# Expert blocks in three host steps instead of four, with the hidden transposes between the two ups of the next pair

## What is computed

```python
scores = sigmoid(xf @ gate_w.T)
_, sel = top_k(scores + expert_bias[None, :], K)          # K = 2 of E = 8
top_scores = take_along_axis(scores, sel, axis=1)
rin = xf[tok_idx] * sc_sorted[:, None]                     # rows in the order of their expert
for e in range(E):
    h = silu(rin @ w1[e].T) * (rin @ w3[e].T)
    out_sorted = out_sorted + m * (h @ w2[e].T)
routed = zeros((N, D)).at[tok_idx].add(out_sorted)
shared = silu(xf @ sw1.T) * (xf @ sw3.T) @ sw2.T
return routed + shared
```

## Time and profile before

| | |
|---|---|
| three runs | 507.58, 510.66, 513.54 us |
| median | 510.66 us |
| the profiled execution | 508.22 us (span of its instructions 506.4 us) |
| busy share of the span | TensorE 89%, VectorE 69%, ScalarE 49%, GpSimd 34% |
| TensorE, mean granted clock | 0.974 of full speed |
| DMA | 42.02 MB, mean 83 GB/s |

### The profile page before, as it was taken

The page is one execution under the profiler, slowest core; times in us unless marked ns, Lnnn a source line. Parts: engine busy times, 40 slices in busy tenths (PEclk is TensorE's granted clock), DMA queues, the critical chain, the costliest instruction groups (busy, mean ns, idle before and its releaser), DMA issues. The chain is left out here.

```text
span 506.4 us, 7287 instructions
## 1 busy us (share of the span) xinstructions
PE 450.3 (89%) x2162; PEld 356.1 (70%) x2162; DVE 347.2 (69%) x994; ACT 247.2 (49%) x479; POOL 173.8 (34%) x181
## 2 busy tenths in 40 slices
PE   2769799589989999999999998998998899899991
PEld 1447588458668776888778786887776688788860
DVE  6968569988486964577978967888778354621173
ACT  2868264223577377455044416360751544955540
POOL 3787232354022333400000000060525015477771
PEclk9999799789999999999999999999999899999997
DMA  8421212002000000980000000142323223346494
GB/s 306 164 80 57 62 33 80 5 20 83 1 1 2 0 1 0 293 218 0 1 2 1 0 2 0 32 136 74 119 71 112 88 79 111 105 150 191 123 380 138
DMA packets 32966, 42.02 MB, mean 83 GB/s; under 512 B 3483, under 2 KB 26781, under 8 KB 32928
## 3 DMA queue, kind: packets, MB, share of 16 engines
q1 hardware_dynamic: 28224, 32.28, 21.0%
q0 software_dynamic: 3744, 8.42, 4.5%
q10 hardware_dynamic: 960, 0.86, 0.5%
HBM read 24.97 MB, written 18.39 MB: 86 GB/s over the span
## 5 line engine op out<-in xcount | busy, mean ns | idle before, releaser
L678 PE MATMUL acc<-w_down,act_s 128*128 128x256 f32 x384 | 91.5, 384 | 0.9 <-DVE act_s L1410 0.9
L678 PEld LDWEIGHTS acc<-w_down,act_s 128*128 128x128 f32 x384 | 73.6, 193 | 12.8 <-DVE act_s L1410 1.3
L654 PE MATMUL ring<-xt_h,up_l 128*128 128x512 f32 x160 | 71.1, 444 | 1.4 <-DVE kv_sum L1490 1.4
L1137 ACT ACTIVATE act_s<-ring 128x512 f32<-128x512 f32 x48 | 28.6, 596 | 73.5 <-PE ring L656 73.3
L655 PE MATMUL ring<-xt_l,up_h 128*128 128x512 f32 x160 | 63.4, 396 | 0.0
L656 PE MATMUL ring<-xt_h,up_h 128*128 128x512 f32 x160 | 63.3, 395 | 0.0
L1625 POOL TENSOR_TENSOR rstd<-var_eps,minus_half 128x4 f32<-128x4 f32 x14 | 14.5, 1039 | 135.7 <-DVE var_eps L1225 135.7
L717 PE MATMUL ring<-up_e,act_s 128*128 x184 | 45.7, 392 | 2.3 <-issue 2.0
L1677 POOL DMA_INDIRECT x_rows<-main_a,slots x32 | 31.1, 972 | 43.7 <-ACT main_a L1158 34.8
L1414 DVE TENSOR_TENSOR act_s<-ring,act_s 128x512 f32<-128x512 f32 x32 | 21.9, 686 | 34.3 <-ACT act_s L1137 16.4
L717 PEld LDWEIGHTS ring<-up_e,act_s 128*128 128x128 f32 x184 | 34.2, 196 | 7.2 <-issue 3.2
(11 more groups left out here) (281 smaller groups left out, 1009.6 us busy)
## 6 DMA issues: line engine op xcount, KB each, us to landing
main_b<-x_rows SPq DMA_DIRECT2D x22, 257.0 KB, 3.0
x_rows<-v_t SPq DMA_DIRECT2D x1, 3983.5 KB, 16.1
up_l<-y_rows SPq DMA_DIRECT2D x5, 512.0 KB, 5.9
stage<-in_w_mlp SPq DMA_DIRECT2D x8, 256.0 KB, 2.6
up_e<-in_w_moe SPq DMA_DIRECT2D x8, 256.0 KB, 2.6
x_rows<-v_t SPq DMA_DIRECT2D x1, 1927.5 KB, 22.4
x_nat<-in_x SPq DMA_DIRECT2D x7, 256.0 KB, 7.9
out_x<-x_nat SPq DMA_DIRECT2D x6, 256.0 KB, 5.0
```

Of the source, the lines that this page charges most:

```text
L654: pe.matmul(out, wl, xh, start=first, stop=False, skip_group_check=True)
L678: last = pe.matmul(acc[t // 2][:, t % 2, :], act_s[n % RING][:, tok], w_down[:, u, :], start=u == 0 and t % 2 == 0, stop=final, skip_group ...
L1137: act.activation(act_s[n % RING][:, :], bank[:, :], ACT.Silu).then_inc(free_sem((step, "A", u)), 1)
```

## The change

The downs of a pair, their copy and their store come one host step earlier, so a pair goes through three steps (x transposed; ups; hidden transposes and downs) instead of four, and step 26 is gone from the list. On TensorE, the hidden transposes of pair n-2 stand between the ups of block 0 and block 1 of pair n-1, and the downs of pair n-2 behind block 1. On ScalarE the copy of the transposed hidden stands ahead of silu, and the copy of the downs (now pair n-2) behind it. GpSimd stores pair n-2.

```diff
-    gather 0 4 5, blk 0 26, moe 3 1, shared 3 0 1, fetch_tile 1 0 1 2 3, gather_tile 1 0 1 2 3"""
+    gather 0 4 5, moe 3 1, shared 3 0 1, fetch_tile 1 0 1 2 3, gather_tile 1 0 1 2 3"""
...
-            def block_ups(n, experts):
...
+            def block_up_rows(n, j, e, bank):
+
+                for c in range(C):
+                    last = pe.matmul(bank[:, j * 2 * P:(j + 1) * 2 * P], x_block_t[n % 2][:, c, j * P:(j + 1) * P],
+                                     up_e[:, bass.ds(e * UP + c * 2 * P, 2 * P)], start=c == 0, stop=c == C - 1)
+                return last
...
                         experts[n - 1] = [block_expert(n - 1, j) for j in range(pair_blocks(n - 1))]
-                        block_ups(n - 1, experts[n - 1])
-                    if 2 <= n <= PAIRS + 1:
+                        freed(pe, (("blk", n - 1), "T"))
+                        key = (("blk", n - 1), "U")
+                        bank = open_bank(key)
+                        last = block_up_rows(n - 1, 0, experts[n - 1][0], bank)
+                        if n >= 2:
+                            transpose_hidden(n - 2)
+                        if pair_blocks(n - 1) == 2:
+                            last = block_up_rows(n - 1, 1, experts[n - 1][1], bank)
+                        close_bank(key, last)
+                    elif n > PAIRS:
                         transpose_hidden(n - 2)
-                    if n >= 3:
-                        block_downs(n - 3, experts[n - 3])
+                    if n >= 2:
+                        block_downs(n - 2, experts[n - 2])
...
+                    if n >= 2:
+                        key = (("blk", n - 2), "H")
+                        bank = full(act, key)
+                        if n >= 4:
+                            full(act, (("blk", n - 4), "D"))
+                        wide = pair_blocks(n - 2) * P
+                        act.activation(hid_block_t[n % 2][:, 0:wide], bank[:, 0:wide], ACT.Copy).then_inc(free_sem(key), 1)
                     if 1 <= n <= PAIRS:
                         bank = full(act, (("blk", n - 1), "U"))
...
-                elif kind == "blk" and part >= 3:
-                    n = part - 3
+                elif kind == "blk" and part >= 2:
+                    n = part - 2
```

More of the change, by code:

```diff
@@ L1180, in _ @@
                                        ACT.Silu).then_inc(block_silu, 1)
-                    if 2 <= n <= PAIRS + 1:
-                        key = (("blk", n - 2), "H")
+                    if n >= 2:
+                        key = (("blk", n - 2), "D")
                         bank = full(act, key)
[L1184 to L1195, removed]
+                        if n >= RESULTS + 2:
+                            blocks = sum(pair_blocks(m) for m in range((n - 2) % RESULTS, n - 2, RESULTS))
+                            act.wait_ge(y_sent[(n - 2) % RESULTS], 16 * blocks)
+                        wide = pair_blocks(n - 2) * D
+                        act.activation(y_blocks[(n - 2) % RESULTS][:, 0:wide], bank[:, 0:wide], ACT.Copy,
                                        scale=gates[:, 3:4]).then_inc(free_sem(key), 1)
```

## The result

| | before | changed |
|---|---|---|
| runs | 507.58, 510.66, 513.54, 505.84 us | 520.65, 517.70, 518.07, 516.16 us |
| median | 509.12 us | 517.88 us |
| profiled execution | 508.22 us (span 506.4) | 520.65 us (span 518.8) |

The change makes the kernel slower: ratio 1.018, 95% interval 1.0135 to 1.0233, that is 9.4 us (6.9 to 11.9) of 509.12. The sign is clear of the noise; whether it is more or less than 2% is not settled.

What follows compares the result with a forecast made beforehand. TensorE's pace and GpSimd's backlog were taken to bound the end together. Delays of 3.4, 4.4, 0.9 and 1.6 made 10.3 us; 3.2 given back left 7.15, so 515.4, plus 2.44 to the median: 517.8 us, range 509.0 to 521.0.

Steps and rivals of the forecast that it cites:

- Two queues at once: At the end GpSimd's backlog holds up to pair 18, TensorE's pace of 3.25 us a pair holds pairs 19 and 20.
- The copy is covered: The second block's ups cover ScalarE's hidden copy with 0.3 us to spare, so the wait costs the matmuls nothing.
- The reads are held by the wait and cost: The downs' new wait stops TensorE's sequencer; two expert-number reads queue behind it, 1.85 us to the next ups' arithmetic.
- Stall 0.44, step 3.69: Each steady expert step on TensorE stalls 0.44 us, so it takes 3.69 us instead of 3.25.
- Ahead of the sends, 1.14: GpSimd's sends start 1.14 us later: 0.7 for one more pair of downs, 0.44 for one stalled interleaved step.
- Step 9, 2.2 us of standing, ups of pair 9 3.4 late: TensorE stands 2.2 us for the hidden copy behind ScalarE's rows; the ups of pair 9 start 3.4 us late.
- Given back by the last steps, 3.2: One step less of latency at the end gives back 3.2 of the 10.3 us of delay.
- The other branch just hidden: The branch behind TensorE's last downs moves by 11.0 us; its additions end at 507.3, just hidden by 508.15.
- The reason given for "held": The wait goes with the downs' register arithmetic, a control instruction, and so stops the sequencer; with a matmul reads would run ahead.
- rival B: The reads run ahead of the wait, steps stay 3.25 us, the kernel is not slower: 509.9 us; chance 0.20.
- Rival D: The main forecast, plus step 9's stand taking TensorE to its lower clock: + 1.7 us, 519.5; chance 0.10.
- Rival C: TensorE never holds GpSimd up, the last store comes 3.4 us earlier: 507.2 us, the ceiling; chance 0.05.

Runs made afterwards that it cites:

- e1: The changed kernel with the next pair's expert numbers read ahead of the wait for the downs, not behind it; ratio to before 1.0043.
- e5: The changed kernel with a small fixed-address matmul put first in the downs' bank to carry the wait for the hidden copy; ratio to before 1.018.
- e9: e1 plus the last four lots of rows in ScalarE's gaps of steps 9 and 10, and single-block hidden transposes ahead of the ups; ratio to before 0.9975.
- e3: e1 plus the rows of the last two tiles filled by ScalarE behind step 9's copies; ratio to before 0.9973.
- e8: As e3, but one of the two tiles' rows behind step 9's copies and the other behind step 10's; ratio to before 0.9979.
- e7: The changed kernel with the hidden transposes behind the ups of both blocks; one run, 533.87 us.

## Why the prediction was right, point by point

The forecast of 517.8 us met 517.88, and that it met it so closely is luck. It went out from a median of 510.66 for the kernel before and added 7.15; the median with the fourth run is 509.12, 1.5 lower, and the change costs 8.8 by the medians, 9.0 in the traces and 9.4 by the ratio. The two errors cancel. The direction, the place and the mechanism held; the size was a fifth too small.

- **Two queues at once** held: after the change GpSimd's backlog is used up by 471 us and TensorE sets the end.
- **The copy is covered**: held, no wait ahead of L732 in a full step, and e1 shows it with the reads out of the way.
- **The reads are held by the wait and cost**: held. On the sequencer of the changed kernel the downs' arithmetic starts at 458.4, the reads at 458.7, the next ups' at 460.4, as the earlier trace rows but now behind the release:

```profile
L732 PEldq FUSED_REGOPS  x2: 46/46/46, 458.4 to 458.5; - x2
...
L708 PEldq TENSOR_LOAD <-block_e x2: 297/416/534, 458.7 to 459.6; - x2
```

- **Stall 0.44, step 3.69**: the term was too small. The ten full steps take 3.68 to 3.94, on average 3.78. The missing 0.09 is the restart: after a stand the ups of one block take 0.96 or 0.97 us (485.95 to 486.92) and not 0.87, because its first record is 478 ns long instead of 379. The row for it was there (the eight of 438.21 in the earlier trace rows take 1.99 us, those of the earlier trace rows 1.89) and I did not price it. From pair 9 to pair 22 that made 7.7 us in place of 6.9.
- **Ahead of the sends, 1.14**: measured 1.36 (sends at t2 + 38.40 against 37.04). The one pair of downs more costs 0.8 rather than 0.7. Step 5 to 6 stood as foreseen (3.72 from ups to ups against 3.25). The restart behind that stand adds the missing 0.1.
- **Step 9, 2.2 us of standing, ups of pair 9 3.4 late**: 1.85 us, and 3.75 late. The stand is shorter since TensorE came later to it: the ups of pair 8 were 1.4 late rather than 1.1, and took the restart on top. The copy ended at t2 + 39.37, which on the clock of the kernel before is 443.54; the prediction has 443.4, though its own terms (442.6, 0.5 and 0.4) add up to 443.5. From there to the ups it took 2.17 us instead of 2.0.

```profile
446.55 0.37 ACT L1183 ACTIVATE k_r<-ring 128x256 f32<-128x256 f32 x1
```

- **Given back by the last steps, 3.2**: too large; it was 2.4 (from the ups of pair 22 to the last store 13.0 us before, 10.6 after). Of the missing 0.8, about 0.3 is the way of the stores: one of them took 1.30 us in place of 0.99. Some 0.2 is lost from the ups of pair 22 to those of pair 23 (3.03 us against 2.81), and another 0.1 is the restart ahead of the downs of pair 22.
- **The other branch just hidden**: held. Its additions and the last store both came later than foreseen (12.6 us for 11.0, and 9.0 for 7.15), and VectorE waited another 1.18 us for the last fetch behind it:

```profile
510.66 1.61 DVE L1248 SCALAR_TENSOR_TENSOR x_nat<-ring,small,x_nat 128x512 f32<-128x512 f32 x2 [1.36 <-PE ring L690]
513.45 0.42 DVE L1583 TENSOR_TENSOR x_nat<-x_nat,gate_pad 128x256 f32<-128x256 f32 x1 [1.18 <-DMA gate_pad<-y_rows]
```

- **The reason given for "held"** was only half right. I had put it on the wait being carried by a control instruction. e5 took that away and the steps stayed as long. So rival B could not have come true on the ground that I gave it; the reads run ahead only if they stand ahead of the wait, as in e1.
- **Rival D** did not come: the granted clock was 1.00 (2.4 GHz) in the stretch from 441 to 507 us of the changed kernel, in spite of the stand of 1.85 us.
- **Rival C's ceiling** of 3.4 us stayed out of reach; e9 got 1.6 of it in its trace.

## What to carry to other kernels

When a pipeline is made one stage shorter, mind not only what the array does during the new wait but what the waiting engine's sequencer still has to do behind it: register reads at 0.65 us each, hidden as long as it runs ahead, come to lie bare behind a fresh wait. Issue such reads ahead of the wait, for the next step; here that one edit took back 8.65 of 9.0 us. And a shorter way pays only where the queue at the end was waiting for it. With the stall gone, three versions (e3, e8, e9) lie 0.2 to 0.3% below the kernel before, each within its interval, so none is shown to be faster; in the traces uncovered copies at the ragged steps gave back part of the 2.6 us (e9).

## What the runs showed that I had not expected

- On TensorE, register arithmetic and reads behind a matmul that waits for a semaphore were held until that wait ended, though they wait for nothing themselves (e5, 470.0 and 470.04, and 24 of 24 pairs).
- The first matmul of the ups after a stand is 478 ns in the records against 379 (all 16 flagged stands of the changed kernel from 405 us on), and what follows the group of four comes 0.09 to 0.1 us later.
- Much of the spread from run to run (505.8 to 513.5 us for the kernel before) can lie outside the changed part. In the profiled executions, with the same work up to there, the transposes of step 2 started anywhere from 402.9 to 409.7 us. Part of it is how long TensorE's clock stays at its lower level of 1.2 GHz near 395. In the changed kernel, around idle spells of 1.25, 0.60, 0.90 and 1.11 us, the granted clock is 0.56 and 0.59 of 2.4 GHz in two stretches,

```profile
396.00:400.00 4.00, 2.89 (x9) 2.19 (x8) 0.79 (x4) 0.60 (x1) 0.00 (x0) 0.56 0.57 158
400.00:404.00 4.00, 4.00 (x12) 3.20 (x11) 0.42 (x1) 2.10 (x3) 0.00 (x0) 0.59 0.00 0
```

against 0.62 and then 0.95 in the kernel before (394 to 398 and 398 to 402). From the ups of pair 0 to the transposes of step 2 it takes 8.95 us there, 10.3 in the changed kernel and 7.4 in e5 and e7, where the granted clock stayed at 1.00 although their idle spells are nearly the same (in e5 1.25, 0.21, 0.90 and 1.08 us). The rest of the 7 us I did not trace. Two profiles of this kernel are best compared by counting from a point ahead of which both do the same.
